# Splat attention and mixture of experts on one core: two projections and four row-maxima move into the first head group, the routing gate's chain moves forward, the task slots are chosen anew, and the last rows are finished singly

## What is computed

```python
xn = layernorm(x)
q, k, v = heads(xn @ Wq.T), heads(xn @ Wk.T), heads(xn @ Wv.T)
scores = einsum('bhid,bhjd->bhij', q, k) / sqrt(16)
std_out = out_proj(softmax(where(mask, scores, neg)))
gauss, dirp = splat_feats(q), splat_feats(k)      # exp and tanh of products with q*q, q and k*k, k
splat = einsum('bhin,bhjn->bhij', amp*qg, kg) + directional * einsum('bhin,bhjn->bhij', amp*qg*qd, kg*kd)
gsa_out = out_proj(softmax(where(mask, scores + sensitivity*splat, neg)))
attn = (1 - blend)*std_out + blend*gsa_out

s = sqrt(softplus(xn @ gate_w.T))                 # 1024 x 16
idx = top_k(s + gate_b, 2); w = gathered s, normalised to sum 1
# each expert takes its first 128 tokens: silu(x W1.T) * (x W3.T) @ W2.T, weighted by w
moe = routed + (silu(xn @ Ws1.T) * (xn @ Ws3.T)) @ Ws2.T
out = x + attn + moe
```

## Time and profile before

| | |
|---|---|
| median of 3 runs | 342.87 us (342.50 to 343.34) |
| the profiled execution | 344.22 us, span 342.4 us |
| busy share of PE, DVE, ACT | 90%, 69%, 59% |
| mean granted TensorE clock | 0.993 of full speed |

### The profile page before, as it was taken

How to read it: one execution, slowest core, us unless ns; L and a number is a source line. 1 busy time by engine, 2 the same in 40 slices (tenths; PEclk the granted TensorE clock), 3 DMA queues, 4 the chain that set the end, 5 groups by cost and what they waited for, 6 DMA issues and landing times.

```text
span 342.4 us, 6091 instructions
## 1 busy us (share of the span) xinstructions
PE 309.8 (90%) x2064; PEld 159.4 (47%) x2064; DVE 236.4 (69%) x735; ACT 201.1 (59%) x300; POOL 39.6 (12%) x59
## 2 busy tenths in 40 slices
PE   0799898899689999999999999999999989999894
PEld 0546633233334445455545554555444544445362
DVE  3948796589988769775775577666955667567424
ACT  1588359766646576656465547465564646647740
POOL 7300000000020000111111111111110023433000
PEclk9999999999989999999999999999999999999999
DMA  7413355234136403554555656654554333222011
GB/s 239 149 23 65 57 88 114 50 68 69 27 63 159 98 5 58 128 143 127 134 141 141 153 133 144 149 137 129 135 145 132 51 58 90 63 62 63 2 61 61
DMA packets 25790, 33.54 MB, mean 98 GB/s; under 512 B 4636, under 2 KB 18556, under 8 KB 25756
## 3 DMA queue, kind: packets, MB, share of 16 engines
q1 hardware_dynamic: 24056, 28.85, 36.6%
q0 software_dynamic: 1536, 4.20, 4.3%
q10 hardware_dynamic: 164, 0.07, 0.1%
HBM read 16.15 MB, written 4.26 MB: 60 GB/s over the span
## 4 chain that ended last, share of the span: by engine, by line
PE 73%; SPq 9%; DVE 9%; ACT 4%; issue 2%; DMA 2%; DVEq 0%
PE ps L1072 19%; PE ps L1042 9%; PE ps L988 9%; PE ps L1054 8%; PE ps L997 7%; PE ps L950 7%; SPq L507 4%; SPq L522 3%; PE ps L861 2%; PE ps L1027 2%; ACT arena_p L829 2%; PE ps L1001 2%; SPq L519 2%; DVE ps L1359 2%; PE ps L871 2%
## 5 line engine op out<-in xcount | busy, mean ns | idle before, releaser
L829 ACT ACTIVATE arena_p<-ps 128x1024 f32<-128x1024 f32 (+1 forms) x192 | 147.4, 808 | 44.0 <-PE ps L1054 28.4
L1359 DVE CUSTOM_DVE_ANT_0 ps<-ps,mask_r 128x128 f32<-128x128 f32 (+3 forms) x128 | 61.4, 504 | 17.7 <-PE ps L950 16.5
L1072 PE MATMUL ps<-arena_p,v_full 128*32 128x512 f32 (+3 forms) x768 | 72.3, 495 | 0.0
L1042 PE MATMUL ps<-stage 98*128 98x512 bf16 (+1 forms) x192 | 50.9, 330 | 5.7 <-ACT arena_p L829 3.4
L950 PE MATMUL ps<-stage 96*128 96x512 bf16 (+3 forms) x160 | 49.3, 344 | 5.8 <-DVE mx L1359 3.5
L1391 DVE TENSOR_REDUCE mx<-ps 128x1 f32<-128x512 f32 x64 | 43.9, 686 | 11.2 <-PE ps L950 10.6
L1054 PE MATMUL ps<-stage 98*128 98x512 bf16 (+1 forms) x192 | 45.4, 326 | 0.1
L611 POOL DMA_INDIRECT wt<-xn_scratch,ids_sb x16 | 15.3, 954 | 221.7 <-PE ps L976 97.1
L1072 PEld LDWEIGHTS ps<-arena_p,v_full 128*32 128x32 f32 x768 | 20.2, 110 | 34.5 <-issue 30.0
L950 PEld LDWEIGHTS ps<-stage 96*128 96x128 bf16 x160 | 15.0, 96 | 35.8 <-issue 26.2
L997 PE MATMUL ps<-arena_o,small 88*128 88x256 f32 x96 | 26.2, 395 | 2.4 <-ACT small L841 0.9
(11 more groups left out here) (199 smaller groups left out, 371.4 us busy)
## 6 DMA issues: line engine op xcount, KB each, us to landing
w_sb<-in_w_dram SPq DMA_DIRECT2D x16, 352.0 KB
stage<-split SPq DMA_DIRECT2D x48, 96.0 KB
stage<-split SPq DMA_DIRECT2D x96, 32.0 KB
stage<-split SPq DMA_DIRECT2D x48, 64.0 KB
arena_o<-in_w_dram SPq DMA_DIRECT2D x16, 176.0 KB
ye_scratch<-wt SPq DMA_DIRECT2D x16, 128.0 KB, 1.9
stage<-split SPq DMA_DIRECT2D x32, 48.0 KB
acc<-in_x_dram SPq DMA_DIRECT2D x2, 512.0 KB, 5.3
```

The lines of the kernel that those rows point to most:

```text
L829: A(to, ps[:, 1 + 2 * s:3 + 2 * s, off:CH], ACT.Exp, scale=SCALE).then_inc(done, 1)
L1042: ins = M(b[:, off:CH], ks[:, pr, h, (jb + s) * P:(jb + s + 1) * P], qs[:, pr, h, ic * CH + off:(ic + 1) * CH], start=True, stop=not diag)
L1072: ins = M(ps[c:c + 2 * HD, 0, off:CH], v_full[:, jb + s, g * GH + h, :], of, start=jb + s == 0, stop=end or last, skip_group_check=last an ...
L1359: return V.tensor_tensor_reduce(row, row, mask_r[:, CH - row.shape[1]:CH], 1.0, NEG, ALU.add, ALU.max, to)
```

## The change

1. `PRO` keeps two of the four `proj1` projections (q of heads 8 to 15, both token halves). The other two (k) become aux tasks in slots 0 and 2 of group 0, evacuated by ACT. Whoever needs them waits through `projected()`.
2. `LATER` goes from 8 to 4: four more maxima of group 0 are `pre` tasks in the first slot, which makes 12.
3. `gate()` stands ahead of the first maxima on DVE; ACT takes Exp between the second and third value copies; the first addition of `plus_one()` comes before the copy of `mT`, the other six operations (`inverse()`) behind it. On PE the first `proj1` now stands in front of the transposes of `shift`.
4. All slots of all groups are filled anew. The tasks are the same but for the two projections and the four maxima.
5. In `END` ACT copies the `rowsh` results, and the last two token blocks are multiplied, added and written one at a time (`tile`, 128x256) instead of as one `out` of 128x512.

```diff
-        PRO += [("proj1", (s, tc)) for s in range(2) for tc in range(NC)]
+        PROJ1 = [("proj1", (s, tc)) for s in range(2) for tc in range(NC)]
+        EARLY_PROJ1 = 2
+        PRO += PROJ1[0:EARLY_PROJ1]
...
-        LATER = 8
+        LATER = 4
...
-                [("pre", ("max", (1, 7, 1)))],
-                [("max2", (0,))],
+                [("pre", ("max", (1, 6, 1))), ("proj1", (1, 1)), ("max2", (0,))],
+                [("pre", ("max", (1, 7, 0))), ("pre", ("max", (1, 7, 1)))],
...
-        END = [("rowsh", 0), ("oTh", 1), ("out", (TC, 1)), ("rowsh", 1), ("out", (TC + 2, 1))]
+        END = [("rowsh", 0), ("oTh", 1), ("out", (TC, 1)), ("rowsh", 1), ("tile", TC + 2), ("tile", TC + 3)]
-        BY_ACT = ("feat1", "hT", "shT")
+        BY_ACT = ("feat1", "hT", "shT", "proj1", "rowsh")
+        def projected(s, tc):
+            t = ("proj1", (s, tc))
+            return (pro_act, emptied_at(t)) if t in PRO else (half_free, free_of(t))
...
+            for n in (TC + 2, TC + 3):
+                sp.wait_ge(aux_free, place(NG, ("tile", n))[2])
+                sp.dma_start(out[n * P:(n + 1) * P, :], acc[:, n, :]).then_inc(y_out, 16)
...
-            for n in range(NT // 2):
-                evacuate(("v", n))
+            evacuate(("v", 0))
+            evacuate(("v", 1))
             act.wait_ge(gate_dve, 1)
             A(g_[2][:, :, :], g_[1][:, :, :], ACT.Exp, scale=-1.0).then_inc(gate_act, 1)
+            evacuate(("v", 2))
+            evacuate(("v", 3))
+            if EARLY_PROJ1:
+                evacuate(PROJ1[0])
             shift_rows(act, -1, 0, 0)
-            evacuate(("proj1", (0, 0)))
             act.wait_ge(gate_dve, 2)
             A(g_[4][:, :, :], g_[3][:, :, :], ACT.Ln).then_inc(gate_act, 1)
-            evacuate(("proj1", (0, 1)))
-            evacuate(("proj1", (1, 0)))
+            for t in PROJ1[1:EARLY_PROJ1]:
+                evacuate(t)
             act.wait_ge(gate_dve, 3)
             A(g_[10][:, :, :], g_[11][:, :, :], ACT.Sqrt).then_inc(gate_act, 1)
-            evacuate(("proj1", (1, 1)))
...
+                            elif kind == "proj1":
+                                bank, count, _ = place(g, (kind, a))
+                                act.wait_ge(aux_full, count)
+                                from_proj(1, *a, ps[:, bank, :], half_free)
...
+                elif kind == "tile":
+                    pe.wait_ge(half_free, place(NG, ("rowsh", 1))[2])
+                    ins = M(b[:, 0:D], oT[:, 1, a * P:(a + 1) * P], wt[:, 3, 1, :], start=True, stop=True)
...
+            gate()
             for t in max0:
                 aux(-1, t)
-            gate()
+            plus_one()
             aux(-1, ("shift", 0))
+            inverse()
             for t in PRE1[0:2]:
                 aux(-1, t)
-            plus_one()
-            for t in PRE1[2:5]:
-                aux(-1, t)
             softplus()
-            for t in PRE1[5:]:
+            for t in PRE1[2:]:
                 aux(-1, t)
```

More of the change, by code:

```diff
@@ new lines, in bass_splat_attention_moe_layer @@
+                [("route", 3)],
+                [("max", (1, 5, 1)), ("rest", 4), ("max", (1, 6, 0))],
+                [("max", (1, 6, 1))],
+                [("route", 4)],
+                [("max", (1, 7, 0)), ("max", (1, 7, 1))],
+                [],
+                [("route", 5), ("shift", 1)],
+                [],
+            ],
+            [
+                [("rest", 5), ("max2", (0,))],
+                [("p1", 4), ("max2", (1,)), ("route", 6)],
+                [],
+                [("max", (0, 2, 0))],
@@ L294, in bass_splat_attention_moe_layer @@
-            [
-                [("max2", (0,)), ("max2", (1,))],
-                [("rest", 6), ("shT", 2), ("rest", 7), ("sy", 2)],
+                [],
+                [("route", 7)],
+                [("oT", 1), ("p1", 5), ("max", (1, 2, 0)), ("max", (1, 3, 0))],
+                [("max", (0, 4, 0)), ("max", (0, 4, 1))],
+                [],
+                [("sgu", 0), ("shift", 0), ("max", (0, 5, 0))],
+                [("oT", 0), ("third", 4), ("max", (0, 5, 1)), ("max", (0, 6, 0)), ("weights", 0)],
@@ L852, in _ @@
                                 part1(a)
+            for kind, a in END:
+                if kind == "rowsh":
+                    bank, count, _ = place(NG, (kind, a))
+                    act.wait_ge(aux_full, count)
+                    A(oT[:, 1, CH + 2 * a * P:CH + 2 * (a + 1) * P], ps[:, bank, 0:2 * P], ACT.Copy).then_inc(half_free, 1)
         @block.tensor
@@ L1021, in aux @@
                             half = (n - TC) // 2
-                            pe.wait_ge(aux_free, place(NG, ("rowsh", half))[2])
+                            pe.wait_ge(half_free, place(NG, ("rowsh", half))[2])
                         else:
@@ L1118, in _ @@
                     prologue(n_v + 3 + n // 4)
+                elif t[0] == "shift" and EARLY_PROJ1:
+                    prologue(n_p)
                 aux(-1, t, 0)
@@ L1371, in aux @@
                     return
-                if kind in ("feat1", "square", "p0", "p1", "weights", "hT", "shT"):
+                if kind in ("proj1", "feat1", "square", "p0", "p1", "weights", "hT", "shT", "rowsh"):
                     return
```

252 lines of the change are left out of this document (123 added, 129 removed).

## The result

The changed kernel takes 339.31 us (median of 20 executions, 336.4 to 341.3 but for three at 341.5, 342.0 and 404.0), against 342.12 for the kernel before on the same chip: ratio 0.9902, 95% interval 0.9885 to 0.992, that is 2.7 to 3.9 us less. The forecast was 2.6 less, at the low edge of that. The size is about right; the experiments will show that the terms it was summed from are not.

What follows compares the result with a forecast made beforehand. PE was taken to bound groups 1 to 6, DVE to set the pace before. The terms 0 + 1.6 + 0.2 + 0 + 0.8 gave 2.6 us off, forecast 340.3 us from a median of 342.87, range 338.4 to 342.3.

Steps and rivals of the forecast that it cites:

- The start of the loop: Before group 0's slots: first exp at 50.5 to 51.2 instead of 53.48, 2.3 to 3.0 us earlier.
- Nothing bought at 63.6: Third pair of group 0: starts at 63.9 against 63.60, net 0 on PE; bounds 0.45 won to 1.3 lost.
- Both anchors: Group 0: `max2` waits for group 1's rows until 56.8; SP issues the shift rows no earlier than 61.19.
- DVE's lead of 0.9: Group 0's rest and routing: DVE finishes `at_slot` 0.9 us earlier, at 95.7, bringing 1.6 on PE at `route` 7.
- the waits only change place: Lower bound of DVE's lead: 0 us, which would leave 0.7 won on PE.
- the 1.88 us in front of 93.35: PE's wait for DVE's maxima before `route` 7, expected to go because group 1's slots hand DVE less at a time.
- The clock: At 99 to 102, granted clock 0.50: if it stays up 1.5 us come back; 0.2 added in the likeliest case.
- The rival that gave 338.6 by the clock: Denser group 1 keeps the clock at 1.00 through 99 to 102: 4.3 us off in all; chance 0.15.
- DVE's lead of 1.3: The larger DVE lead, in us, that the rival with the clock staying up assumed; its chance 0.15.
- Groups 1 to 6: From 102 to 319, PE busy 211.1 of 217.0 us: 0 gained, bounds 0.8 either way.
- the last of my own signs: The prediction is wrong if groups 1 to 6 take other than 217 +- 0.8 us.
- The end: Last products and adds: ACT's copy and single tiles finish the last add 0.8 us earlier; bounds 0.3 to 1.1.

Runs made afterwards that it cites:

- The last version: New slots of groups 1 to 7 and new end put on the kernel before, its front and group 0 kept: 337.75 us, ratio 0.9884.
- the front alone: Kernel before with two projections and four maxima moved, new gate order, new slots of groups 0 and 1: 345.16 us, ratio 1.0082; once more 344.76, 1.009.
- the changed kernel with fillers: Changed kernel plus 16 unread matmuls, 8 before the first standard scores, 8 in group 0's last shift: 341.31 us, ratio 0.9937 against the kernel before.

## Why the prediction was right, and where it was not

The last version is the partner for the changed kernel that the prediction lacked: they differ in the front and group 0 alone, and their prologues run in step but for some tenths (first statistics 5.07 and 5.05). Against it:

- **The start of the loop: right in sign, too small.** First exp 48.20 against 51.82, 3.6 us earlier (2.3 to 3.0 expected).
- **Nothing bought at 63.6: right, for another reason.** The third pair starts at 63.49 against 62.56, 0.9 later (0.3 expected, bounds 0.45 won to 1.3 lost). Both anchors that I had named were wrong: `max2` at 55.84 did not wait for group 1's rows, and SP issued the shift rows at 59.75, not 61.19; in front of that it had nothing left to issue from 58.7 on and stood waiting for `mT`. PE itself is the limit: busy 11.94 of 12.70 us up to there. I had kept SP's times fixed, though its rows of group 1 went out 2.4 earlier in this execution.
- **DVE's lead of 0.9: the step that failed.** `at_slot` is done at 96.27, and `route` 7 stands at 96.42, against 95.69 in the partner: 0.7 later instead of 1.6 earlier. (The partner has group 1's new slots. From the first statistics, `route` 7 stands at 91.4 here and at 91.1 to 92.2 in the profiles with the old ones: no gain either.) The term's lower bound, "the waits only change place", was still too good. DVE's busy time from 5 to 96, partner first:

```profile
5.00:96.00 91.00, 75.67 (x451) 38.40 (x452) 73.90 (x248) 60.54 (x87) 5.34 (x15) 1.00 0.40 82
```

```profile
5.00:96.00 91.00, 79.15 (x438) 38.48 (x438) 73.05 (x245) 58.33 (x84) 5.31 (x15) 0.96 0.39 80
```

  DVE has done 0.85 us less by then. From 40 on, the partner's waits of half a microsecond and more on PE are the old one of 2.69 and four of 0.63 to 1.54, 6.7 us together. Here there are six, 8.2 us together. For the projection in slot 0 I had 0.7, and it is 2.07; for `max2` I had 1.7 until group 1's rows are in, and it is 1.17 behind the second projection. The other four, 0.87 for the first maxima and 0.54, 1.76 and 1.77 later, stood in my sum as some tenths:

```profile
52.01 0.69 DVE L1424 TENSOR_REDUCE mx<-ps 128x1 f32<-128x512 f32 x1 [2.07 <-PE ps L972]
...
62.51 0.57 DVE L1392 CUSTOM_DVE_ANT_0 ps<-ps,mask_r 128x384 f32<-128x384 f32 x1 [1.76 <-PE ps L972]
...
70.79 0.69 DVE L1424 TENSOR_REDUCE mx<-ps 128x1 f32<-128x512 f32 x1 [1.77 <-PE ps L972]
```

  Each projection holds the maxima back for its 2 to 3 us on PE. Where DVE is the bound and PE is its supplier, moving 4 us of PE work from ahead of the loop into it starves DVE, even if PE gains the same 4 us ahead. That is my reading of these waits; no run moves the projections without new slots for group 0. And the 1.88 us in front of 93.35, which I expected to go, went only there: `shift` 1 now stands behind `route` 5 in its slot, and PE waits 1.87 for it at 87.39.
- **The clock.** I expected the fall at 99 to 102 to stay. It went, and two came, which together cost about 1 us by the executions with and without them, 0.3 to 0.5 by the profiles: in the front's profile without any fall the third copy of the value products lies at 100.64, in its other at 101.14, here at 100.91; with the long fall it is 102.29. The rival that gave 338.6 by the clock is right that the clock is worth something: the six executions at 1.00 took 336.4 to 338.6. It did not decide the median, and DVE's lead of 1.3, which it also needed, did not exist. The Trainium skill ("TensorE: Matmul & The Clock Gate", "Part 1: The HAM clock gate") has idleness bring the throttle back; the falls here and those at 161.5 and 284.5 stand right behind stops of 1.65 to 1.87 us, in agreement. But it is not certain: the front's first profile has waits of 1.66 and 1.87 at the same places, and the clock is 1.00 up to the last microsecond.
- **Groups 1 to 6, "0, bounds 0.8": mis-sized.** The new slots of groups 2 to 7 alone give 3.1 us. I took a busy share of 97% for a ceiling near zero. 5.9 us of idle stood in the earlier trace rows, and I did not look at which instructions they stand before; the group of `y` and `sy` would have shown 2.4 us of it before one kind (L997), a wait that a plan can remove; nearly all of it is in front of `sy`, in five places. By the last of my own signs (groups 1 to 6 take 217 +- 0.8 us) this step was wrong. And the busy time itself is not incompressible: it shrank by 1.36 with the same matmuls.
- **The end: right.** 1.1 measured (0.4 to 1.9), 0.8 expected. The copy on ACT takes 0.38 and the two adds 0.88, where I had 0.42 and twice 0.42; the time from last add to end fell from 2.5 to 2.2 on top.

The sum was 0 + 1.6 + 0.2 + 0 + 0.8 = 2.6. By the runs it is about -0.6 to -1.6 for the front and group 0 beside the new late slots (ratios and medians against the last version), 3.1 for groups 2 to 7 (and perhaps something for group 1), 1.1 for the end. An error of about 3 us down was met by one of 3 up: that the total fits is luck.

## What to carry to other kernels

A right total proves no term: time the parts alone, since here the part that the change is named after costs 2.8 us alone and is likely the one to leave out. When tasks are placed among the work of a bound engine, list its small waits by the instruction that they stand before, at 97% busy too. Here they gathered before a product whose input goes through another engine's copy, and the longest went not by more distance but by taking another task away from in front of the producer. And when work is moved across the engine that supplies the bound one, ask what the bound engine is fed with meanwhile.

## What the runs showed of the hardware

- **A wait can cost more than its length.** Behind 14 of the 20 PE waits of 1.6 to 1.9 us in the fourteen profiles the granted clock went to its lower level (1.2 GHz; 0.50 to 0.54 over the stretch) for about 3.5 us, once for 6.8; behind the other six it did not, or not at once. Where PE waits for DVE anyway two falls cost 0.3 to 0.5 us by the profiles and about 1 by the executions; in the middle of group 6, with PE the bound, the longer stop and its fall cost 2.65 us, and near 160, in the changed kernel with fillers, 3.4 (14.60 us from one copy of the value products to the next instead of 11.20). A kernel with such a place scatters: the front alone took 341.7 to 347.3.
- **Stops without a cause in the profile.** 1.38 us (before 161.57) and 1.65 (before 161.09) between two matmuls of one transposition, and at `sy` 4 the growth from 0.7 to 1.8. In the longest case there DVE and ACT stand idle too, waiting for two transpositions that by the profile ended on PE at 281.16 and 281.51:

```profile
283.43 0.21 DVE L1427 COPY mT<-ps 16x128 bf16<-16x128 bf16 x1 [0.76 <-PE ps L964]
283.48 0.38 ACT L851 ACTIVATE small<-ps 88x256 f32<-88x256 f32 x1 [2.73 <-PE ps L964]
```

  So it is PE's results that come late, not the copies. In the two cases near 160 a packet of the queue that the page of the profile calls q8, instruction, had been moved about 1 us ahead of the stop (18 or 19 such packets in a run, 0.29 to 0.31 MB together). The Trainium skill ("Runtime: NRT & Kernel Launch", "Instruction fetch mechanics") says that instructions come in blocks of 16 KiB and that crossing a block is mostly hidden; 0.29 MB in 18 packets agrees with the size. But at `sy` 4 the nearest packet came 1.5 to 4 us after the stop, and most packets in every run passed without one. What makes these stops, and why the new front makes the one at `sy` 4 longer, stays open.
